# Aggregating over the graph with the adjacency as the stationary operand, two frames ahead

## The reference

```
h = x                                    # x: (B=64, N=128, D=256)
for _ in range(3):
    a_in = a_out = einsum('nm,bmd->bnd', adj, h)
    av = concatenate([a_in, a_out], axis=-1)
    z  = sigmoid(lin(av, w3) + lin(h, u3))
    r  = sigmoid(lin(av, w4) + lin(h, u3))
    hv = tanh(lin(av, w5) + lin(r * h, u5))
    h  = (1 - z) * h + z * hv
return layernorm(x + h)
```

## Time and profile before

| | |
|---|---|
| median of 3 runs | 761.15 us (760.79 to 761.39) |
| the profiled execution | 761.69 us, span of its instructions 758.8 us |
| PE busy | 746.4 us, 98% |
| PE weight loads | 632.4 us, 83% |
| DVE busy | 544.5 us, 72% |
| ACT busy | 388.7 us, 51% |
| POOL busy | 72.8 us, 10% |
| mean granted TensorE clock | 0.995 |

### The profile page before, as it was taken

One profiled execution on the slowest core, in us unless ns is written; L12 is line 12 of the kernel. 1 busy time (PEld: TensorE's weight loads), 2 busy tenths in 40 slices (PEclk: granted clock), 3 DMA queues, 4 the chain that ended last, 5 costly groups with the idle time before them and its releaser, 6 DMA issues.

```text
span 758.8 us, 10474 instructions
## 1 busy us (share of the span) xinstructions
PE 746.4 (98%) x3681; PEld 632.4 (83%) x3681; DVE 544.5 (72%) x858; ACT 388.7 (51%) x647; POOL 72.8 (10%) x91
## 2 busy tenths in 40 slices
PE   9999999999999999999999999999999999999994
PEld 7888888888888888888888888888888888888883
DVE  6657787777767776887677667887677756887675
ACT  5545454455556444545566544545466645444454
POOL 0000111100100011110100001120000000211003
PEclk9999999999999999999999999999999999999998
DMA  8122312233453322223355242222335432111222
GB/s 309 33 38 37 90 28 34 39 44 80 117 123 67 103 39 38 39 37 58 63 121 134 67 92 32 38 33 35 64 63 130 125 66 38 30 31 31 43 45 103
DMA packets 208425, 51.82 MB, mean 68 GB/s; under 512 B 201232, under 2 KB 201360, under 8 KB 208400
## 3 DMA queue, kind: packets, MB, share of 16 engines
q1 hardware_dynamic: 208256, 51.24, 31.3%
q10 hardware_dynamic: 144, 0.26, 0.1%
HBM read 18.95 MB, written 8.39 MB: 36 GB/s over the span
## 4 chain that ended last, share of the span: by engine, by line
PE 98%; DVE 1%; DMA 1%; POOL 0%; issue 0%; ACT 0%; ACTq 0%; SPq 0%; POOLq 0%
PE ps_g L327 17%; PE ps_g L326 17%; PE ps_g L328 17%; PE ps_a L351 11%; PE ps_v L326 11%; PE ps_v L327 11%; PE ps_v L328 11%; PE ps_g L408 1%; DMA x_in<-in_x_rows 1%; PE ps_v L408 0%; DVE dz L648 0%; DVE hT L658 0%; DVE dz L643 0%; PE ps_a L482 0%; DVE stats L756 0%
## 5 line engine op out<-in xcount | busy, mean ns | idle before, releaser
L523 ACT ACTIVATE ps_v<-ps_v,bias 128x512 f32<-128x512 f32 x96 | 63.6, 662 | 199.9 <-PE ps_v L328 199.9
L328 PE MATMUL ps_g<-aT_hi,wt_hi 128*128 128x512 f32 x376 | 146.3, 389 | 0.0
L326 PE MATMUL ps_g<-aT_hi,wt_lo 128*128 128x512 f32 x376 | 146.3, 389 | 0.0
L327 PE MATMUL ps_g<-aT_lo,wt_hi 128*128 128x512 f32 x376 | 146.3, 389 | 0.0
L643 DVE TENSOR_TENSOR dz<-ps_v,hT 128x512 f32<-128x512 f32 x64 | 44.3, 692 | 103.6 <-ACT ps_v L523 103.6
L553 ACT CAST rh_hi<-rh 128x512 fp32r<-128x512 f32 x96 | 59.6, 621 | 78.1 <-DVE rh L663 78.1
L561 ACT ACTIVATE z<-ps_g,bias 128x512 f32<-128x512 f32 x96 | 64.2, 687 | 47.5 <-PE ps_g L328 46.4
L638 DVE TENSOR_TENSOR aT_lo<-ps_a,aT_hi 128x512 fp32r<-128x512 f32 x96 | 62.4, 673 | 28.9 <-ACT aT_hi L508 28.8
L328 PEld LDWEIGHTS ps_g<-aT_hi,wt_hi 128*128 128x128 f32 x376 | 70.6, 188 | 14.6
L326 PEld LDWEIGHTS ps_g<-aT_hi,wt_lo 128*128 128x128 f32 x376 | 70.6, 188 | 14.6
L327 PEld LDWEIGHTS ps_g<-aT_lo,wt_hi 128*128 128x128 f32 x376 | 70.6, 188 | 14.6
(11 more groups left out here) (78 smaller groups left out, 1185.2 us busy)
## 6 DMA issues: line engine op xcount, KB each, us to landing
hn<-hb SPq DMA_DIRECT2D x736, 32.0 KB, 2.0
x_in<-in_x_rows SPq DMA_DIRECT2D x16, 512.0 KB, 4.9
xT<-in_x_cols SPq DMA_DIRECT2D x15, 512.0 KB, 4.4
out<-y SPq DMA_DIRECT2D x15, 512.0 KB, 2.7
wide<-in_w_t SPq DMA_DIRECT2D x3, 512.0 KB, 6.0
xT<-in_x_cols SPq DMA_DIRECT2D x2, 256.0 KB, 4.7
out<-y SPq DMA_DIRECT2D x2, 256.0 KB, 2.0
square<-in_u_t ACTq DMA_DIRECT2D x1, 256.0 KB, 2.8
```

What stands on the lines that cost most here:

```text
L326: nc.tensor.matmul(dst, lhs_lo, rhs_hi, start=first, stop=False, skip_group_check=True)
L327: nc.tensor.matmul(dst, lhs_hi, rhs_lo, start=False, stop=False, skip_group_check=True)
L328: return nc.tensor.matmul(dst, lhs_hi, rhs_hi, start=False, stop=last, skip_group_check=True)
L523: nc.scalar.activation(ps_v[:, oc, :], ps_v[:, oc, :], ACT.Tanh, bias=bias[:, BV, oc:oc + 1]).then_inc(v_ready, 1)
```

## The change

Three things change together.

- **The aggregate.** `adjT` is split in high and low parts once and becomes the weight; the state with nodes on the partitions is split too (`hn_high` on ACT, `hn_low` on DVE) and moves through it in 512 columns: 6 matmuls, `product` twice. The result then has nodes on the partitions. The first two aggregates of the program keep the old form.
- **The way back.** DVE transposes the aggregate in 32 x 32 blocks out of PSUM (`transpose_a`, into `ab`), SP writes `ab` to DRAM (`park_a`) and reads it back into its partitions (`move_a`, 4 DMAs), and only then ACT and DVE split it (`a_high`, `a_low`). The state's own blocks now go over DRAM as well (`park_h`, `move_h`), 5 DMAs in place of 16.
- **The order.** The aggregate is computed two frames ahead in place of one. `add_x` moves from POOL to DVE. The loads of node-layout rows move to other places of SP's order: `reload_rows`.

```
+            def reload_rows(i, q):
                 oi, oq = (i, q - 2) if q >= 2 else (i - 1, q + 2)
-                sp.wait_ge(a_ready, 2 * frames(oi, oq))
+                sp.wait_ge(hn_lo_ready, split_aggregates(oi, oq))
                 load_rows(i, q)

-            def move(i, j):
+            def park_h(i, j):
                 sp.wait_ge(hb_ready, frames(i, j))
+                sp.dma_start(turned_h[j % 2], hb[j % 2][:, :, :]).then_inc(hb_parked[j % 2], DMA)
+
+            def move_h(i, j):
+                sp.wait_ge(hb_parked[j % 2], parks(i, j))
                 for n in range(QUADS):
-                    for f in range(QUADS):
-                        sp.dma_start(hn[j % SLOTS][n * BLK:(n + 1) * BLK, :, :, f * BLK:(f + 1) * BLK],
-                                     hb[j % 2][f * BLK:(f + 1) * BLK, :, :, n, :]).then_inc(moved[j % SLOTS], DMA)
+                    sp.dma_start(hn[j % SLOTS][n * BLK:(n + 1) * BLK, :, :, :, :].rearrange("r f c b i -> r f (c b i)"),
+                                 turned_h[j % 2][:, n, :].rearrange("(f r) x -> r f x", f=QUADS))\
+                      .then_inc(moved[j % SLOTS], DMA)
+
+            def park_a(i, j):
+                sp.wait_ge(ab_ready, split_aggregates(i, j))
+                sp.dma_start(turned_a, ab[:, :, :]).then_inc(ab_parked, DMA)
+
+            def move_a(i, j, first=False):
+                sp.wait_ge(ab_parked, DMA * split_aggregates(i, j))
+                if not first:
+                    sp.wait_ge(a_lo_ready, 2 * frames(*frame_before(i, j)))
+                for f in range(QUADS):
+                    sp.dma_start(aT[f * BLK:(f + 1) * BLK, :, :],
+                                 turned_a[:, f, :].rearrange("(n r) x -> r n x", n=QUADS)).then_inc(a_moved, DMA)
...
-            def frame(i, j, carry, refill):
-                if j < 2:
-                    load(i, j + 2)
+            def frame(i, j, carry, refill, second=True):
                 if carry and j < SLOTS:
                     store(i - 1, j)
+                bi, bj = frame_before(i, j)
                 if carry or j > 0:
-                    bi, bj = frame_before(i, j)
-                    move(bi, bj)
-                    if refill and bj >= FR - SLOTS:
-                        load_cols(bi + 1, bj % SLOTS)
+                    park_h(bi, bj)
+                if second:
+                    park_a(*after(i, j, 2))
+                if carry or j > 0:
+                    move_h(bi, bj)
+                if second:
+                    move_a(*after(i, j, 2))
+                if (carry or j > 0) and refill and bj >= FR - SLOTS:
+                    load_cols(bi + 1, bj % SLOTS)
+                if refill and j in (4, 5):
+                    reload_rows(i + 1, j - 4)
+                elif refill and j == FR - 1:
+                    reload_rows(i + 1, 2)
+                elif carry and j == 0:
+                    reload_rows(i, 3)
...
         # PE
+            def aggregate(i, j, first=False):
+                pe.wait_ge(hn_hi_ready, split_aggregates(i, j))
+                pe.wait_ge(hn_lo_ready, split_aggregates(i, j))
+                if first:
+                    pe.wait_ge(adj_lo_ready, 1)
+                    pe.wait_ge(a_lo_ready, 2 * frames(0, 1))
+                else:
+                    pe.wait_ge(ab_ready, split_aggregates(*frame_before(i, j)))
+                for k in range(2):
+                    cols = slice(k * ROWS, (k + 1) * ROWS)
+                    product(ps_a[:, k, :], adjT_hi[:, :], adjT_lo[:, :], hn_hi[:, cols], hn_lo[:, cols],
+                            True, True).then_inc(a_ready, 1)
...
+            def frame(i, j, carry):
+                second_half(i, j, carry)
+                aggregate(*after(i, j, 2))
+                update_product(*after(i, j, 1), carry)
+                candidate(i, j)
...
         # ACT
+            def a_high(i, j):
+                act.wait_ge(a_moved, QUADS * DMA * split_aggregates(i, j))
+                nc.scalar.copy(quads_first(aT_hi), by_block(aT)).then_inc(a_hi_ready, 2)
+
+            def hn_high(i, j):
+                if j < SLOTS:
+                    act.wait_ge(x_loaded[j % 2], DMA * (turn(i, j) - 1))
+                    src = x_in[j % 2]
+                else:
+                    act.wait_ge(moved[j % SLOTS], moves(i, j - SLOTS))
+                    src = hn[j % SLOTS]
+                nc.scalar.copy(hn_hi[:, :], flat(src[:, :, :, :, :])).then_inc(hn_hi_ready, 1)
...
                 for oc in range(C):
                     act.wait_ge(rh_ready, C * frames(i, j) - 1 + oc)
                     nc.scalar.copy(rh_hi[:, oc, :], rh[:, oc, :]).then_inc(rh_hi_ready, 1)
+                if second and not first:
+                    hn_high(*second)
...
         # DVE
+            def transpose_a(i, j, first=False):
+                dve.wait_ge(a_ready, 2 * frames(i, j))
+                if not first:
+                    dve.wait_ge(a_moved, QUADS * DMA * split_aggregates(*frame_before(i, j)))
+                nc.vector.transpose(ab[:, :, :].rearrange("p q x -> p (q x)"),
+                                    ps_a[:, :, :].rearrange("p k x -> p (k x)")).then_inc(ab_ready, 1)
...
                 for c in range(C):
                     times_r(i, j, c)
                     if first and c == 0:
                         weight_low(W3)
-                    if following and not first:
+                if second and not first:
+                    hn_low(*second)
+                if following and not first:
+                    for c in range(C):
                         h_low(*following, c)
                 rh_low(i, j, 0)
                 rh_low(i, j, 1)
...
                 if before and following:
                     transpose_blocks(bi, bj, carry or bj >= 2)
+                if second:
+                    transpose_a(*second, first=first)
+                if following and not first:
+                    a_low(*following)
                 if j >= FR - 2:
                     statistics(i, j - (FR - 2))
                 elif carry and j < SLOTS - 2:
                     statistics(i - 1, j + 2)
-                if following:
-                    for hf in range(2):
-                        a_low(*following, hf)
+                if before and SLOTS <= bj < 2 * SLOTS:
+                    add_x(bi, bj)
```

More of the change, by code:

```diff
@@ L69, in build @@
     QUADS = P // BLK
[L70 removed]
+    LINE = C * GB * BLK
+    WIDE = QUADS * LINE
     DMA = 16
     assert N == P and C == 2 and GB == 4 and ROUNDS * GB * SLOTS == B
+    turned_h = [nc.dram_tensor(f"turned_h{k}", [P, QUADS, LINE], F32).ap() for k in range(2)]
+    turned_a = nc.dram_tensor("turned_a", [P, QUADS, LINE], F32).ap()
     ctx = ExitStack()
@@ L110, in build @@
         shift = [sb(f"shift{q}", [P, GB]) for q in range(SLOTS)]
-        x_in = [sb(f"x_in{k}", [P, GB, D]) for k in range(2)]
-        hb = [sb(f"hb{k}", [P, C, GB, QUADS, BLK]) for k in range(2)]
+        x_in = [sb(f"x_in{k}", [P, QUADS, C, GB, BLK]) for k in range(2)]
+        hb = [sb(f"hb{k}", [P, QUADS, LINE]) for k in range(2)]
+        ab = sb("ab", [P, QUADS, LINE])
+        aT = sb("aT", [P, QUADS, LINE])
         z = [sb(f"z{k}", [P, C, ROWS]) for k in range(2)]
         y = [sb(f"y{k}", [P, GB, D]) for k in range(2)]
+        x_first = y
+        adjT_hi = sb("adjT_hi", [P, N], F32R)
+        adjT_lo = sb("adjT_lo", [P, N], F32R)
+        hn_hi = sb("hn_hi", [P, WIDE], F32R)
+        hn_lo = sb("hn_lo", [P, WIDE], F32R)
         hT_hi = sb("hT_hi", [P, C, ROWS], F32R)
@@ L291, in _ @@
             load_wide(W3)
-            load_rows(0, 1)
+            load_first_rows(1)
             load_cols(0, 1)
             sp.dma_start(square[1][:, :, :], u5_t).then_inc(w_loaded[U5], DMA)
+            load_rows(0, 2)
             load_cols(0, 2)
+            load_rows(0, 3)
             load_cols(0, 3)
+            park_a(0, 2)
+            move_a(0, 2, first=True)
             EARLY = SLOTS
-            for j in range(EARLY):
+            for j in range(1, EARLY):
                 frame(0, j, False, False)
             with sp.Fori(1, ROUNDS) as i:
-                load(i, 0)
-                load(i, 1)
                 for j in range(EARLY, FR):
@@ L309, in _ @@
             for j in range(EARLY, FR - 1):
-                frame(last, j, True, False)
+                frame(last, j, True, False, second=j + 2 < FR)
             for q in range(SLOTS - 1):
@@ L336, in dense, with first_aggregate @@
                 return done
[L338 to L344, removed]
+            def first_aggregate(j):
+                pe.wait_ge(rows_first[j], DMA)
                 for hf in range(2):
@@ L564, in frame @@
                     weight_high(U5)
-                if following:
-                    split_first_half(*following)
+                    act.wait_ge(adjT_loaded, DMA)
+                    nc.scalar.copy(adjT_hi[:, :], adjT[:, :]).then_inc(adj_hi_ready, 1)
+                    for hf in range(2):
```

(10 more changed lines are left out.)

164 lines of the change are left out of this document (102 added, 62 removed).

## The result

| | median us | ratio to before [95% interval] |
|---|---|---|
| before | 760.97 (760.74 to 761.39) | |
| after | 791.19 (791.03 to 791.95) | 1.0398 [1.0384, 1.0412] |
| predicted | 765.5 (751 to 782) | |

The direction was the likelier one of the forecast (chance 0.53); the size was not: the forecast was 25.7 us too low. The profiled execution took 791.22 us, its span is 789.4.

What follows compares the result with a forecast made beforehand. The prediction took PE's matmuls to bound the kernel. From 761.7 us it added 7.5 for three crossings with late reloads, took off 4.4 for other aggregates, added 1.3 for the start, less 0.5 for the median: 765.5 us (751 to 782).

Steps and rivals of the forecast that it cites:

- the stall: On DVE ahead of hn_low, waiting for ACT's copy hn_hi: 1.7 us in each frame.
- Without anything else the next X follow 15.68 apart: Frames 10, 11, 0, 1: successive starts of hn_low (X) lie 15.68 us apart, DVE's need with statistics.
- X is at least V + 7.87: Frames 11, 0, 1, 2: normalise delays ACT's second sigmoid, so hn_low starts at least 7.87 us after V.
- The reload: x_in for frames 2 and 3, issued at X + 11.8, landing in 5.3, 2.5 us late in frames 0 and 1.
- the mean step s: From one hn_low start to the next where the x_in load is late: 18.2 us, bounds 15.7 and 20.0.
- Bandwidth is not the cause: At the late reload: 2 MB go out in some 5 us, and DMAs have moved 406 GB/s.
- The clock, priced at nothing: PE's clock falling in the new gaps: two gaps of some 2.5 us in 187 were priced at nothing.
- its end gives nothing: add_x leaving POOL ends its hold on DVE (2.88 for 0.68 us), hidden behind PE, so no gain.
- the second rival: The state's trip over DRAM is late in every frame: 780 us and more, chance 0.14.
- The dear-DVE rival: DVE's strided or PSUM instructions (transpose_blocks, transpose_a, a_low) cost twice the price: 875 us, chance 0.05.
- Neither effect: Rival: ACT's copy comes out at 0.60 and the reload is early: 747 us or less, chance 0.03.
- The start: transpose_a of frame 2 ahead of DVE's first update: D 3.2 us late, PE feels 1.3 (bounds 0 and 3.2).

Runs made afterwards that it cites:

- the kernel with both edits: Kernel after, with the two reload_rows of a crossing issued ahead of park_h and normalise moved on ACT behind a_high: 749.25 us, 0.9862 of before.
- the experiment on it: Kernel after with normalise at the end of ACT's frame, plus reload_rows issued ahead of load_cols: 764.26 us, 1.0033 of before.
- the early loads: Kernel after, with SP issuing the two reload_rows of a crossing ahead of park_h: 780.12 us, 1.0251 of before.
- single fixes: Kernel after with one edit each: reload_rows ahead of park_h, 780.12 us; normalise moved on ACT behind a_high, 778.44 us.
- another kernel: Kernel after with normalise at the end of ACT's frame and reload_rows ahead of load_cols: 764.26 us, 1.0033 of before.

## Why the prediction was wrong in size

- **The aggregate, PE's frame, DVE's instructions** were right: 1.36 and 14.96 us; the stall 1.64 (said 1.7); the copy of 1024 elements 1.04 in the median, 1.08 at most (said 1.05); DVE busy 629.3 (said 635). The strided runs and the PSUM source cost DVE nothing extra: `a_low` 1.18 us, `transpose_a` 1.21, beside 1.23 for `hn_low`. DVE's own step in the crossing, bare in the kernel with both edits, is 15.55 (said 15.68).
- **The step that failed: "Without anything else the next X follow 15.68 apart", and with it "X is at least V + 7.87"** (V is the time at which tanh would let DVE start). For `normalise` I took ACT's push from the earlier trace rows, where the shift was ready. But the change puts the stall, `hn_low`, `transpose_a` and `a_low` ahead of `statistics`, at the end of DVE's frame, and so the shift became a wait: 18.1 to 18.2 per step by itself, where I had 16.0 and 15.68. I costed what `statistics` delays, and not who waits for it. First and fourth step came out 2.2 and 2.1 above, 12.8 us over three crossings.
- **The reload: mechanism right, one term too small.** It is late in frames 0 and 1, six times, and five times issued at X + 11.84 to 11.87 (said 11.8). The landing was 6.9 in the mean of the six, not 5.3. Once the issue came at X + 12.97, because the four issues of `move_h` took 2.87 us in place of 1.77. With both, the mean step s is 20.0, my upper bound, and 11.0 us more than forecast over three crossings.
- **"Bandwidth is not the cause" was wrong.** I held 2 MB against the best rate in a row. Windows of the kernel after, at the load and at a stretch of large packets:

```profile
397.00:399.00 2.00, 2.00 (x11) 1.65 (x10) 1.87 (x3) 1.34 (x3) 0.55 (x2) 1.00 1.12 212
401.00:403.00 2.00, 2.00 (x9) 1.63 (x10) 1.26 (x2) 1.75 (x4) 0.00 (x0) 1.00 0.96 272
...
432.00:434.00 2.00, 2.00 (x10) 1.64 (x10) 2.00 (x5) 0.00 (x0) 0.00 (x0) 1.00 0.99 408
```

  The DMA engines are busy all the time (share 1.12 and 0.96) at 212 and 272 GB/s, where block reads, `xT`, `x_in` and a store overlap; when mainly the parked tiles are written they move 408 at a share of 0.99. The rate that goes with a full share depends on what they carry, so the share column, not the last, tells whether there is room. That the order of two loads moves the landing by 1.7 us in the mean (the experiment on it) bears this out. By the estimate from the Trainium skill's fit (DMA: Bandwidth & Descriptors, Anatomy of one DMA) the reload would land in 3.2 us. The trace doesn't agree: the 14 loads land in 6.1 us in the median, the six late ones in 6.0 to 8.1.
- **The sum.** 12.8 + 11.0 = 23.8, what the crossings took above the forecast. In the two middle steps either wait alone hides most of the other. Had the load landed in 5.3, the middle steps would have been 18.2 all the same, since the ring takes 18.1.
- **The clock, priced at nothing.** It did fall, to 0.50 for some 3.4 us behind a gap of 2.56 us, which I had held too short. The price came out right by luck, for my reason was wrong: the clock fell, but with the gaps filled the time stayed within the intervals.
- **`add_x`: "its end gives nothing"** was wrong in the sense that counts. Back on POOL it costs 30 us in the new order, because the hold falls on `times_r`, ahead of `hn_lo`, which has 0.5 us of slack by the prediction's own count: 2.2 less 0.5 is 1.7, measured some 1.85 a frame. As a term of the sum it did no harm: DVE's 15.03 in frames 5 to 8 was forecast to be hidden, and those frames measure 14.96.
- **The trip of the state over DRAM**, the second rival, was never late: `park_h` lands in 2.7 as predicted, and ACT waits for no `hn`. The dear-DVE rival fell with the 1.2 us instructions. "Neither effect" (747 or less) is what the mended kernels come near, 749 us with both moves and 743 with the statistics moved too.
- **The start**: DVE's first update comes 15.61 us behind the first sigmoid r (31.11 less 15.50), before 12.40 (26.18 less 13.78): 3.2 later, as forecast. The sigmoid itself starts 1.7 later than before, but that can't be put down to the change: it starts at 13.07 to 16.04 in the profiles of kernels whose code up to there is that of the kernel after. So the 1.9 outside the crossings lie within what the start of a single profile varies by, and what PE felt of the 3.2 wasn't settled by a run.

## What to carry to other kernels

When work is inserted ahead of an instruction, list who waits for its result, engine by engine, and follow the ring until it comes back: here statistics, shift, normalise, r and `hn_low` closed at 18.1 us, and moving `statistics` alone was worth 28 us on top of the early loads. Two waits that hide behind each other make single fixes look poor (11 and 13 us of 42), so try them together before dropping either. Before a transfer is called cheap, read the DMA share of the stretch in which it will run, and not the best rate seen elsewhere.

## What the runs showed of the hardware that was not expected

- **DMA engines busy all the time at little more than half the rate.** In 396 to 404 us of the kernel after 893 of 1237 packets are below 2 KB; in 431 to 434.5 it is 23 of 279:

```profile
DMA packets 1237, 2.19 MB, mean 273 GB/s; under 512 B 134, under 2 KB 893, under 8 KB 1237
...
DMA packets 279, 1.05 MB, mean 300 GB/s; under 512 B 23, under 2 KB 23, under 8 KB 279
```

  The second stretch is idle for its first microsecond and then runs at some 410. That the packets' size is the reason, rather than the mix of reads and writes in DRAM, is argued from these rows and was not isolated.
- **A short gap can halve the clock, and doesn't always.** After 2.56 us without a matmul the next 3.4 us were granted 0.50, and with 12 matmuls in the gap it stayed at 1.00; in another kernel it fell behind 1.89 us and stayed up behind 2.86.
- **POOL suffers from DVE as DVE from POOL.** The power of 4 elements per partition (line 937) takes 1.43 to 1.50 us where it starts while DVE is in an instruction on two SBUF operands (in the kernel after, line 787), and 1.04 where it starts beside one that reads PSUM or while DVE is idle. In the ring of 18.1 us this is on the path. No run moved that instruction alone.
